# Where the softmax sums divide: probabilities before the transposes, or the heads' outputs behind them

## What is computed

```python
q = _l2norm(q) * q_scale
k = _l2norm(k) * k_scale
sim = jnp.einsum('bhid,bhjd->bhij', q, k) * SCALE
...
sim = jnp.where(causal[None, None], -neg, sim)
attn = jax.nn.softmax(sim, axis=-1)
out = jnp.einsum('bhij,bhjd->bhid', attn, v)
out = out.transpose(0, 2, 1, 3).reshape(b, n, h * dh)
return out @ Wout
```

## Time and profile before

| | us |
|---|---|
| median of 3 runs | 587.52 (585.92 to 587.97) |
| span of the profiled execution, first to last instruction | 585.1 |
| PE busy in it | 466.3 (80%) |
| DVE busy | 427.7 (73%) |
| ACT busy | 394.1 (67%) |
| POOL busy | 324.0 (55%) |

### The profile page before, as it was taken

One profiled execution on the slowest core, in us unless ns is written; L12 is line 12 of the kernel. 1 busy time (PEld: TensorE's weight loads), 2 busy tenths in 40 slices (PEclk: granted clock), 3 DMA queues, 4 the chain that ended last, 5 costly groups with the idle time before them and its releaser, 6 DMA issues.

```text
span 585.1 us, 12616 instructions
## 1 busy us (share of the span) xinstructions
PE 466.3 (80%) x2947; PEld 366.5 (63%) x2948; DVE 427.7 (73%) x1508; ACT 394.1 (67%) x1133; POOL 324.0 (55%) x489
## 2 busy tenths in 40 slices
PE   0664253888778798997998999999799899989986
PEld 0553132667667667775776777777577677777764
DVE  3875262666666289779779887887977988788785
ACT  2451243555555697896897798689689779968864
POOL 2236788900000268947847875784785787577140
PEclk9996656999999999999998999899999999989998
DMA  8910112121121000000000000100000010010010
GB/s 225 355 58 28 45 41 67 37 60 54 51 57 49 29 0 13 8 2 20 18 0 12 24 0 0 31 4 0 18 18 0 9 27 0 0 31 5 2 37 11
DMA packets 28588, 21.20 MB, mean 36 GB/s; under 512 B 3560, under 2 KB 25744, under 8 KB 28432
## 3 DMA queue, kind: packets, MB, share of 16 engines
q1 hardware_dynamic: 25696, 16.65, 9.6%
q0 software_dynamic: 2048, 4.20, 2.4%
q10 hardware_dynamic: 816, 0.03, 0.1%
HBM read 12.48 MB, written 8.39 MB: 36 GB/s over the span
## 4 chain that ended last, share of the span: by engine, by line
PE 32%; issue 18%; DVE 16%; POOL 14%; ACT 13%; DMA 3%; another core or an unknown queue 1%; SPq 1%; ACTq 1%; DVEq 1%; POOLq 0%
POOL slot_x L406 6%; PE bank L946 5%; PE bank L948 5%; PE bank L947 5%; ACT arena_b L651 4%; ACT arena_a L598 3%; PE bank L1068 3%; PE bank L1075 3%; PE bank L1058 3%; DVE arena_b L889 3%; DVE arena_b L873 2%; POOL rpow L419 2%; PE bank L1120 2%; DMA arena_b<-in_L_ffn_wu_dram 2%; DVE ssq L850 2%
## 5 line engine op out<-in xcount | busy, mean ns | idle before, releaser
L651 ACT ACTIVATE arena_b<-arena_b,nmx 128x130 f32<-128x130 f32 (+1 forms) x256 | 115.0, 455 | 21.9 <-DVE nmx L889 19.1
L889 DVE CUSTOM_DVE_ANT_0 arena_b<-bank,bias 128x130 f32<-128x130 f32 (+1 forms) x256 | 81.3, 355 | 24.9 <-PE bank L1075 17.1
L873 DVE TENSOR_SCALAR arena_b<-arena_b,rden 128x130 f32<-128x130 f32 (+1 forms) x256 | 90.0, 397 | 4.6
L419 POOL TENSOR_TENSOR rpow<-ssm,mhalf 128x8 f32<-128x8 f32 x32 | 53.0, 1655 | 56.7 <-DVE ssm L854 56.6
L1075 PE MATMUL bank<-arena_a 128*128 128x258 f32 x256 | 76.7, 382 | 0.0
L432 POOL TENSOR_TENSOR arena_b<-arena_b,rnorm 128x512 f32<-128x512 f32 x64 | 67.2, 1051 | 8.4 <-POOL rnorm L422 3.8
L1068 PE MATMUL bank<-ident,arena_b 128*128 128x128 f32 x384 | 67.5, 285 | 3.3 <-DVE arena_b L873 3.1
L416 POOL TENSOR_TENSOR rnorm<-ssm,mhalf 128x8 f32<-128x8 f32 x32 | 52.7, 1647 | 7.4 <-DVE ssm L854 7.1
L587 ACT ACTIVATE arena_b<-bank 128x512 f32<-128x512 f32 x64 | 38.2, 597 | 25.7 <-PE bank L948 14.9
L1068 PEld LDWEIGHTS bank<-ident,arena_b 128*128 128x128 f32 x384 | 42.4, 142 | 16.7 <-issue 8.6
L1058 PE MATMUL bank<-probT,arena_a 128*64 128x256 f32 x256 | 48.6, 414 | 3.9 <-DVE arena_r L864 3.2
(11 more groups left out here) (212 smaller groups left out, 1307.5 us busy)
## 6 DMA issues: line engine op xcount, KB each, us to landing
slot_x<-probT SPq DMA_DIRECT2D x4, 640.0 KB, 7.7
arena_b<-slot_x SPq DMA_DIRECT2D x40, 64.0 KB, 1.8
slot_y<-arena_b SPq DMA_DIRECT2D x40, 64.0 KB, 1.6
arena_b<-in_L_ffn_wd_dram SPq DMA_DIRECT2D x1, 1024.0 KB, 9.6
arena_b<-in_L_attn_Wkv_dram SPq DMA_DIRECT2D x1, 1024.0 KB, 8.6
arena_b<-in_L_attn_x_dram SPq DMA_DIRECT2D x8, 128.0 KB, 2.1
out_dram<-arena_b SPq DMA_DIRECT2D x8, 128.0 KB, 1.8
arena_b<-in_L_attn_Wq_dram SPq DMA_DIRECT2D x1, 512.0 KB, 6.4
```

Of the source, the lines that this page charges most:

```text
L419: gp.tensor_tensor(rpow[:, j, :], ssm[:, j, :], mhalf[:, 0:HEADS // 2], ALU.pow).then_inc(g.pw, 1)
L651: sc.activation(prob[:, h % 4, c], sim[h % 2][:, c], ACT.Exp, scale=-1.0, bias=nmx[:, h % HEADS, t:t + 1], accum_out=den[:, h % HEADS, t:t ...
L873: ve.tensor_scalar(pr, pr, rden[:, h % HEADS, t:t + 1], None, ALU.mult).then_inc(g.pn, 1)
L889: ve.tensor_tensor_reduce(out=sim[h % 2][:, c], in0=bank[h % 2][:, c], in1=bias[:, c], scale=-SLOPES[h], scalar=3e38, op0=ALU.add, op1=ALU ...
```

## The change

The probabilities stay undivided. L873 on DVE goes, and PE's transposes wait for the exponentials alone. In the step in which PE transposes an odd head, and behind these transposes, it now makes four small fp32 products (two heads, two halves of the tokens): the stationary operand is the reciprocal of each token's sum, repeated over 64 columns, the moving one the identity. They leave each head's 256 reciprocals, repeated over 64 partitions, in the second half of bank 4 (`rpair`). ACT copies them to SBUF (`rows`), behind the side jobs and ahead of its copy of `probT[1]`, where its rounding of `opair` is gone. DVE multiplies `opair` by `rows` in the place where it took the rest, and the result `oT` is plain fp32. The product with `Wout` is one fp32 product in place of three fp32r ones, so `wo` is loaded as it is and its split goes. POOL's copy of the null keys' columns becomes a multiplication by `rden`.

```diff
-                        pool.wait_ge(g.pn, TB * (HEADS * b + h + 1))
+                        pool.wait_ge(g.rd, HEADS * b + h + 1)
...
-                            gp.tensor_copy(pnull[:, t, 4 * q:4 * q + 4].rearrange("p (h n) -> p h n", n=2),
-                                           two[:, :, c0:c0 + NNULL]).then_inc(g.pnc, 1)
+                            gp.tensor_tensor(pnull[:, t, 4 * q:4 * q + 4].rearrange("p (h n) -> p h n", n=2),
+                                             two[:, :, c0:c0 + NNULL], bc(rden[:, 2 * q:2 * q + 2, t], NNULL),
+                                             ALU.mult).then_inc(g.pnc, 1)
...
-                    h = head_at(part, s, 5)
-                    if h is not None and h % 2:
-                        p = h // 2
-                        act.wait_ge(g.pvd, PAIRS * b + p + 1)
-                        if part != "first" or p >= 2:
-                            act.wait_ge(g.oread, PAIRS * b + p - 1)
-                        sc.activation(oT[p % 2][0], opair, ACT.Copy).then_inc(g.ohi, 1)
                     for job in behind(part, b, s, 1):
                         side_out(*job)
                     h = head_at(part, s, 3)
                     if h is not None and h % 2 == 1:
+                        p = h // 2
+                        act.wait_ge(g.rps, PAIRS * b + p + 1)
+                        if part != "first" or p >= 2:
+                            act.wait_ge(g.odone, PAIRS * b + p - 1)
+                        sc.activation(rows[p % 2][:], rpair, ACT.Copy).then_inc(g.rev, 1)
                         act.wait_ge(g.ptps, HEADS * b + h + 1)
...
-            ve.tensor_tensor(wo[1][:], raw_o, wo[0][:].bitcast(F32), ALU.subtract).then_inc(g.wraw_lo, 1)
...
-                        dve.wait_ge(g.ohi, PAIRS * b + p + 1)
-                        ve.tensor_tensor(oT[p % 2][1], opair, oT[p % 2][0].bitcast(F32),
-                                         ALU.subtract).then_inc(g.olo, 1)
+                        dve.wait_ge(g.pvd, PAIRS * b + p + 1)
+                        dve.wait_ge(g.rev, PAIRS * b + p + 1)
+                        if part != "first" or p >= 2:
+                            dve.wait_ge(g.oread, PAIRS * b + p - 1)
+                        ve.tensor_tensor(oT[p % 2][:], opair, rows[p % 2][:], ALU.mult).then_inc(g.odone, 1)
...
-                        dve.wait_ge(g.rd, HEADS * b + h + 1)
-                        for t, c in ((0, slice(0, K0)), (1, slice(K0, KS))):
-                            pr = prob[:, h % 4, c]
-                            ve.tensor_scalar(pr, pr, rden[:, h % HEADS, t:t + 1], None, ALU.mult).then_inc(g.pn, 1)
...
-                        if part != "first" or p >= 1:
-                            pe.wait_ge(g.olo, PAIRS * b + p)
+                        pe.wait_ge(g.rev, PAIRS * b + p + 1)
...
-                        pe.wait_ge(g.pn, TB * (HEADS * b + h + 1))
+                        pe.wait_ge(g.exp, TB * (HEADS * b + h + 1))
...
+                        if h % 2:
+                            p = h // 2
+                            pe.wait_ge(g.rd, HEADS * b + h + 1)
+                            if part != "first" or p >= 1:
+                                pe.wait_ge(g.odone, PAIRS * b + p)
+                            for t in range(TB):
+                                for half in range(2):
+                                    hh = 2 * (p % PAIRS) + half
+                                    ins = te.matmul(rpair[half * DH:(half + 1) * DH, t * P:(t + 1) * P],
+                                                    rden[:, hh, t:t + 1].to_broadcast([P, DH]), ident[:],
+                                                    start=True, stop=True)
+                            ins.then_inc(g.rps, 1)
...
-                        pe.wait_ge(g.olo, PAIRS * b + p + 1)
-                        three(bank[6][:, 0:SEQ], [x[:, p % PAIRS, :] for x in wo], oT[p % 2], p == 0,
-                              p == -1).then_inc(g.oread, 1)
+                        pe.wait_ge(g.odone, PAIRS * b + p + 1)
+                        te.matmul(bank[6][:, 0:SEQ], wo[:, p % PAIRS, :], oT[p % 2][:], start=p == 0,
+                                  stop=p == -1).then_inc(g.oread, 1)
```

22 lines of the change are left out of this document (10 added, 12 removed).

## The result

| | us |
|---|---|
| changed kernel, median of 4 runs | 612.92 (611.99 to 614.55) |
| kernel before, on the same chip, median of 4 runs | 587.75 (585.92 to 588.64) |
| ratio, with 95% interval | 1.0433 (1.0408 to 1.0458) |
| span of the profiled execution after | 611.3 (before 585.1: +26.2) |

The change makes the kernel 4.3% slower. The table of stretches of the changed kernel has the answer to the earlier trace rows: one middle batch (first line), the last batch up to its last scores, and from there to the end. The columns are those of rows 1.

The account below looks back on a forecast made before the run. PE's queue was taken as the bound in most steps. Six middle batches +14.4, first batch +3 and last +4.5 make +21.9 on the 585.1 us span, 607.0; the median lies 2.4 above: 609, range 586 to 633.

Parts of the forecast that it names:

- Part 1: Four small products on PE: 0.73 us a pair, 0.44 for passes and 0.29 for turning from full-width products and back.
- rival a: The two heads' small products on PE do not overlap: 1.17 us a pair, 633 us; chance 0.12.
- Part 2: Product with `Wout` on PE: three fp32r passes become two fp32 ones, +0.08 us a pair.
- Part 3: Divisions leave DVE, 9.6 us a batch; PE's waits in steps 7, 8 and 10 go, about 4 us back.
- Part 4: ACT's copy of `rpair` waits for PE; waits of 0.8 in step 3 and 1.5 in step 13 stay.
- Part 5: Small products wait for DVE's product of the pair before: 0.9 us in step 9, 0.15 in step 7.
- The middle batches: Each of the six middle batches of the attention stage takes 51.2 us, +2.4; together +14.4.
- The last batch: Last batch of the attention stage: +4.5 us, with steps 7, 9 and 11 longer by 1.1, 1.3 and 1.3.
- The rest, the drain: Drain after the last scores: -1.2 us for divisions and a step behind the values' product, +1.1 for additions: nothing.
- The start: Time before the first scores, with the split of `wo` gone: nothing, bounds 0 and -2 us.
- Rival (b): DVE was the bound everywhere and PE's waits vanish: middle batch 47.8 us, kernel 578; chance 0.12.
- Rival (c): The pieces cancel: turning costs nothing, small products 0.44 us a pair, kernel 583 to 592; chance 0.13.

Follow-up runs that it names:

- e8: The kernel before without the division of the probabilities, plus the four small products on PE with their result unread; 604.43 us, ratio 1.0333.
- e3: The kernel before without L873, the division of the probabilities, and nothing added to PE or ACT; 561.34 us, ratio 0.9573.
- e1: The changed kernel with DVE writing each reciprocal over 64 columns and two full-width products replacing the four small ones; 614.75 us, ratio 1.0455.
- e7: e1 with DVE's product of a pair moved ahead of the odd step's bias and maximum; 606.98 us, ratio 1.0381.
- e9: The changed kernel with two full-width transposes as small products, the short reciprocals spread by one DVE copy a pair; 580.04 us, ratio 1.011.
- e10: e9 with DVE, not ACT, copying the spread reciprocals out of their bank, and DVE's product earlier; 577.23 us, ratio 1.0067.
- e6: The changed kernel with two transposes of 128-column reciprocals, DVE's product earlier, and DVE, not ACT, copying the spread reciprocals; 590.96 us, ratio 1.0106.
- e11: e10 with the copy that spreads the reciprocals on POOL; 600.77 us, ratio 1.0455.
- e12: e10 with DVE's copy and product ahead of its side jobs and of the copy of `probT[0]`; 579.9 us, ratio 0.9895.

## Why the prediction was right, and where it was off

The median came out at 612.9, where 609 was forecast with a range of 586 to 633. The mechanism held: PE's queue is the bound in most steps, and what is added there is paid. The terms below that were too small add up to 5.8 us, and the start hides 1.5 of them.

- **Part 1, the small products: right.** 0.73 a pair was forecast and 0.78 is read, in the changed kernel and by e8 less e3 in steps 0 and 1; the net over the kernel is 0.70. Of it, the turn was put at 0.29 and measures 0.33 by e1. The upper end (rival a, 1.17 a pair) is excluded. The Trainium skill ("TensorEngine Tiling (Array Packing)", Key Properties) states that changing the tiling mode drains the engine, and by that rule each visit pays; the trace agrees, with 0.33 us for the way there and back.
- **Part 2, `Wout`: right in size.** 0.08 was forecast for each. In step 1 of a middle batch, from the last transpose ahead of the product to the first behind it, it is 0.54 us in the changed kernel and 0.47 before (the starts of the product alone, 0.43 in rows 2 and 0.44 now, hide this: the fp32r one starts earlier behind the transposes). The changed kernel's steps 1, 5 and 11 are 0.06 to 0.09 longer than e8's.
- **Part 3, the divisions: right.** About 4 us a middle batch were to come back. e3 gives 3.4 a middle batch and 25 over the kernel, and the places were the ones named: in the changed kernel, step 8 of the batch of rows 1 falls by 2.3 and step 10 by 1.0, and the three steps 8 to 10 together from 10.7 to 9.3, with the small products' 0.7 and the new wait in them. That saving is small against the 76 us that DVE works less over the kernel (427.7 before, 352.0 after), because DVE's work stood beside PE's. DVE's busy time in a batch came to 31.0, where 29 was forecast. One thing the forecast did not see: the batch that it read is one of two in which the clock stays up behind the wait in step 8. In the other four middle batches step 8 takes 7.0 to 7.3 us and step 10 only 2.4 (last section), and the changed kernel has neither the wait nor the slow products. It made no difference to the sum, since all six batches took 48.8 to 48.9.
- **Part 4, ACT's copy: right in size, not in place.** The pause of 1.7 us is still there once a middle batch, on another line (L632 in place of L587), and PE loses it in step 12 now: that step is 0.8 longer, and steps 13 and 14 are 0.3 and 0.7 shorter. The wait for the keys' copy in step 3 shrank by 0.3, where I had kept all 0.8 of it.
- **Part 5, the wait for DVE: a term that was too small.** In step 9 I put 0.9 and it measures 1.2 as the profile counts, and the step is 1.9 longer than before, with the small products' 0.7 in it.
- **The middle batches: 0.4 too small, 2.1 us over six.** The average was forecast at 51.2 and came to 51.6. The small products' 0.05 a pair, eight times, is as much as that. The waits that were kept come to the 3.5 of the sum, 0.3 more in step 9 and that much less elsewhere.
- **The last batch: too small by 0.7.** Step 11 took 1.9 us more and not 1.3. The sum of the other steps was met within 0.2.
- **The rest, the drain: the step that failed.** I had it at nothing and it measures +2.8. The timeline of PE behind the last scores, of the changed kernel, shows it:

```profile
597.14 0.49 PE L1060 MATMUL bank<-ident,arena_b 128*128 128x128 f32 x3
598.23 0.66 PE L1070 MATMUL bank<-ident,rden 128*64 128x128 f32 x8 [0.59 <-DVE rden L866]
599.36 0.81 PE L1050 MATMUL bank<-probT,arena_a 128*64 128x256 f32 x3 [0.47 <-ACT rows L632]
...
601.35 0.49 PE L1060 MATMUL bank<-ident,arena_b 128*128 128x128 f32 x3
602.15 0.66 PE L1070 MATMUL bank<-ident,rden 128*64 128x128 f32 x8 [0.31 <-DVE oT L862]
...
603.28 0.81 PE L1050 MATMUL bank<-probT,arena_a 128*64 128x256 f32 x3
```

Twice the small products wait for DVE's operations of the pair before (its product, and the reciprocal behind it). Both times the product with the values begins only when ACT has copied `rpair` behind them (598.92 to 599.30 the first time), and its second head's half 0.64 later, behind ACT's second copy, that of `probT[1]`; the second time a small transpose of the null keys is in between. From the first transpose to the values' product it is 2.2 and 1.9 us, where before it was 1.1 and 0.9. I had counted the small products and one copy once, and forgotten part 5's wait in the drain, though with the stage empty nothing covers it. The -1.2 that I set against them was not there either: without the divisions (e3) the drain is 0.2 shorter. The small products alone (e8 less e3) cost 1.4 in it, and the rest of the change, with ACT's copy ahead of DVE's product, the other 1.6.

- **The start: the bound held, the value not.** I took 0 out of 0 to -2; it is -1.5. What makes it isn't shown. The earlier end of the weights' split would do it, but among the kernels that have no split the first scores start anywhere from 198.9 to 200.9 us (e7 and e1), and with the split from 200.0 to 201.1 (e3 and the kernel before), so part of it may be luck.

Rival (b) is refuted: it asked for PE's waits to vanish, and by e3 the waits that stay cost a middle batch about 4 us even with no division at all (45.4 against the 41.3 that PE's queue takes by itself). Rival (c) needed a turn that costs nothing. In the chances, a third of (c)'s 0.13 is 0.04 and not 0.03.

What stays open: why PE's saving is only partly seen in e9 was read off its waits, not tested by a run. In e10 the long wait in step 8 is in three of the six middle batches followed by slow products (below). These batches are 1.3 us longer, so it makes 4 us of the 19 by which e10 missed its expectation; the other 15 are not explained by a run.

## What to carry to other kernels

Before moving work from one engine to another, count who is the bound step by step. 76 us of DVE work were worth 25 us, since they lay beside PE's queue, and 0.78 us in PE's queue, 64 times, was worth 45 of its 50 us. Work that spreads a small result should be priced by the operation at its new width: spreading first and then computing (reciprocals of 128 columns) cost six times the plain one, while computing first and spreading with a copy cost a third of it. A two-engine handover that feeds a third (PE to ACT to DVE) can be collapsed onto the engine that uses the result. Here that was worth 2% where DVE had the long reciprocals and nothing clear where it had short ones, and what it is worth to put it ahead of that engine's side jobs isn't shown. Which wait then takes its place is to be read again at each step.

## What was not expected of the hardware

- **A reciprocal's time grows steeply with its columns.** 2 columns take 161 ns and 128 take 949 on DVE (groups above), while a copy to 256 columns takes 294. In e9, a copy and two short reciprocals replace two long ones: 0.62 us in place of 1.90 for a pair.
- **The same copy can take four times as long beside POOL's work.** In e10 its mean is 455 ns, and in one place it took 1.14 us, with POOL's scaling beside it (as the two of L873 took 1.57 in place of 0.55 in the earlier trace rows). All ten copies of e10 that began while POOL's scaling L432 ran took 0.96 to 1.15 us, while the 21 beside the norms (L416 and L419) took 0.29 to 0.30. In e9 the copy began ahead of the scaling wherever they had more than 0.15 us in common, and all 64 took 0.29 to 0.30:

```profile
405.01 1.04 POOL L432 TENSOR_TENSOR arena_b<-arena_b,rnorm 128x512 f32<-128x512 f32 x1 [0.16 <-POOL rnorm L416]
405.06 1.14 DVE L857 COPY rwide<-rden 128x256 f32<-128x256 f32 x1
```

- **A stall can be followed by slow products, and what they cost depends on the bound.** The stretch behind e10's wait in step 8, and an undisturbed one of the same batch:

```profile
413.50:416.80 3.30, 3.30 (x15) 2.83 (x16) 2.27 (x9) 0.80 (x5) 2.98 (x8) 0.57 0.09 25
420.00:423.00 3.00, 3.00 (x21) 2.63 (x20) 2.38 (x10) 1.89 (x5) 2.36 (x5) 1.00 0.18 45
```

The granted clock is 0.57 behind the wait, near the lower level of 1.2 GHz against 2.4 elsewhere, and products take twice as long. Step 9 of this batch takes 3.01 us, against 2.00 in the batch before it, whose step 8 is as long (5.30 us). So the same stall is followed by slow products in one turn of the loop and not in the next. The kernel before does it too: behind the same wait of 2.1 us in step 8, four of its six middle batches have a stretch like this one, of the third batch (clock 0.55), and two, that of rows 1 among them, have none.

```profile
318.50:322.30 3.80, 3.80 (x20) 2.73 (x19) 3.46 (x15) 2.03 (x7) 2.14 (x5) 0.55 0.25 69
```

There it costs next to nothing: steps 8 to 10 take 10.8 to 11.0 us with the slow products and 10.7 without, because the waits behind them go (step 10 takes 2.38 in place of 3.51), and the batch is 48.8 to 48.9 either way. In e10 the batch is 48.4 with them and 47.1 without.

- **A pause with no engine named moves with the program.** It is on L587 before and on L632 in the changed kernel, both of ACT, and in e6 on DVE's copy of the reciprocals (in four turns on ACT's L631 at the same moment), each about once for each turn of the loop:

```profile
ACT rows L632 <- remote: 12.0, 7, 1.8
```

```profile
DVE arena_b L867 <- remote: 9.0, 6, 1.5
```

In e7 such a line stands once in the attention stage, and in e9, e10 and e11 not at all. These three ran on another chip, where the kernel before too took 572.8 us. It wasn't profiled there, but their first stage speaks for the chip: no experiment touches it beyond the split of `Wout`, all other kernels have such lines on its splits of weights (4 to 12 us on L532 or L533), and these three have none there either. In e12, which ran on a third chip and differs from e10 in the order of DVE's work alone, the first stage has 4.4 us of them again, and the attention stage only short ones (five that come to 1.7 us together, and one of 0.8). For the attention stage that leaves open which of the two does it.
